# One order string of steps against another in a two-context, twelve-block kernel

## What is computed

```
for level in 0..3:
    x = x + cross_attention_level(norm(x), context)     # L0x, L1x, L2x, L3x
    x = attention_level(norm(x))                        # L0a (linear), L1a (softmax, band), L2a (linear), L3a (gated scan)
    x = x + experts_level(norm(x))                      # L0f, L1f, L2f, L3f (routed experts; L2f has an attention inside)
```

## Time and profile before

| | |
|---|---|
| Median of three runs | 2558.8 us (2552.28 to 2561.77) |
| Span of the profiled execution | 2557.4 us |
| Mean granted TensorE clock | 0.971 |
| PE busy / PEld busy | 2254.9 / 1506.9 us |
| DVE / ACT / POOL busy | 1746.6 / 1368.6 / 774.0 us |
| DMA | 84.14 MB, 33 GB/s |

### The profile page before, as it was taken

The page is one execution under the profiler, slowest core; times in us unless marked ns, Lnnn a source line. Parts: engine busy times, 40 slices in busy tenths (PEclk is TensorE's granted clock), DMA queues, the critical chain, the costliest instruction groups (busy, mean ns, idle before and its releaser), DMA issues.

```text
span 2557.4 us, 62072 instructions
## 1 busy us (share of the span) xinstructions
PE 2254.9 (88%) x26420; PEld 1506.9 (59%) x26556; DVE 1746.6 (68%) x4832; ACT 1368.6 (54%) x2287; POOL 774.0 (30%) x676
## 2 busy tenths in 40 slices
PE   5889999877988888998888888888988889999999
PEld 3556666655565554565655666665656556555666
DVE  5775666577667777676777778777767674556642
ACT  4667676545555665545666544344455544555542
POOL 3323446432342212122222122211223223323443
PEclk9999999989999999999999999999999989999999
DMA  3011313100000000010000000000000102121132
GB/s 115 19 41 34 80 45 75 42 24 9 9 11 14 8 8 6 1 47 10 17 16 10 19 25 25 25 16 17 10 11 16 58 8 71 40 55 54 55 104 62
DMA packets 50452, 84.14 MB, mean 33 GB/s; under 512 B 9536, under 2 KB 24768, under 8 KB 49792
## 3 DMA queue, kind: packets, MB, share of 16 engines
q1 hardware_dynamic: 50176, 80.18, 11.3%
HBM read 77.54 MB, written 2.62 MB: 31 GB/s over the span
## 4 chain that ended last, share of the span: by engine, by line
PE 57%; DVE 25%; ACT 8%; issue 4%; POOL 3%; DMA 1%; SPq 1%; another core or an unknown queue 0%; DVEq 0%; POOLq 0%; ACTq 0%
PE psum L946 6%; PE psum L908 5%; PE psum L904 5%; PE psum L1606 3%; PE psum L463 2%; DVE c_L3x_most L1726 2%; PE psum L1699 2%; DVE c_L2x_mx L2081 2%; PE psum L1984 2%; DVE c_L2x_p L2087 1%; PE psum L471 1%; PE psum L1395 1%; PE psum L1976 1%; PE psum L773 1%; PE psum L778 1%
## 5 line engine op out<-in xcount | busy, mean ns | idle before, releaser
L893 POOL TENSOR_TENSOR c_L3f_h<-c_L3f_h,c_L3f_spread 128x512 f32<-128x512 f32 x96 | 121.3, 1283 | 188.8 <-DMA c_L3f_spread<-scratch 103.1
L471 PE MATMUL psum<-halves_held 128*128 128x512 bf16 x454 | 131.0, 403 | 14.0 <-issue 9.8
L936 DVE TENSOR_TENSOR c_L3f_h<-c_L3f_h,psum 128x512 f32<-128x512 f32 (+1 forms) x112 | 75.9, 682 | 76.5 <-PE psum L908 52.0
L922 ACT ACTIVATE c_L3f_h<-psum 128x512 f32<-128x512 f32 (+1 forms) x112 | 65.5, 594 | 110.2 <-PE psum L904 99.1
L946 PEld LDWEIGHTS psum<-weights,c_L3f_h 128*128 128x128 f32 (+1 forms) x896 | 108.1, 193 | 19.3 <-issue 15.3
L946 PE MATMUL psum<-weights,c_L3f_h 128*128 128x128 f32 (+1 forms) x896 | 112.9, 279 | 0.0
L904 PE MATMUL psum<-c_L3f_xT,weights 128*128 128x512 f32 x208 | 107.4, 601 | 0.0
L908 PE MATMUL psum<-c_L3f_xT,weights 128*128 128x512 f32 x208 | 107.4, 603 | 0.0
L471 PEld LDWEIGHTS psum<-halves_held 128*128 128x128 bf16 x588 | 54.3, 102 | 74.8 <-issue 35.1
L893 POOL TENSOR_TENSOR c_L0f_h<-c_L0f_h,c_L0f_spread 128x512 f32<-128x512 f32 x64 | 82.5, 1313 | 50.4 <-DVE c_L0f_h L936 39.2
L1606 PE MATMUL psum<-c_L3x_qx,c_L3x_kT 32*128 32x256 f32 x512 | 77.1, 427 | 21.1 <-DVE c_L3x_most L1726 17.4
(11 more groups left out here) (640 smaller groups left out, 6520.0 us busy)
## 6 DMA issues: line engine op xcount, KB each, us to landing
c_L0f_spread<-scratch SPq DMA_DIRECT2D x64, 256.0 KB, 5.5
c_L3f_spread<-scratch SPq DMA_DIRECT2D x32, 512.0 KB, 5.3
c_L2f_spread<-scratch SPq DMA_DIRECT2D x64, 128.0 KB, 3.1
c_L3f_spread<-scratch SPq DMA_DIRECT2D x64, 128.0 KB, 5.8
c_L0x_ctxT<-ctxT SPq DMA_DIRECT2D x8, 384.0 KB, 7.8
c_L1x_ctx<-ctx SPq DMA_DIRECT2D x16, 192.0 KB, 2.4
c_L2x_ctxT<-ctxT SPq DMA_DIRECT2D x8, 384.0 KB, 3.6
c_L3x_ctxT<-ctxT SPq DMA_DIRECT2D x8, 384.0 KB, 3.7
```

Source lines behind the costliest of these rows:

```text
L471: nc.tensor.matmul(j.psum[:, bank, :], j.half["ident"], j.half["take"], start=True, stop=True)
L893: nc.gpsimd.tensor_tensor(h, h, j.m["spread"][:, f, :], ALU.mult).then_inc(*j.up("mixed"))
L922: nc.scalar.activation(j.m["h"][P - rows:P, f, :], j.psum[0:rows, 1 + 2 * f % 3, 0:j.tok], ACT.Silu).then_inc(*j.up("silu"))
```

## The change

The string `ORDER` is replaced by another one, and nothing else. Both strings hold the same 8114 steps and the same 9 `+`. The new one is joined from 25 stretches, each taken from one of three orders: the old one and two that were found by search. The digits differ: the old string asks for 588 fillers in all, the new one for 558.

Read step by step, both strings come again and again to the same state (the same steps issued). Between such states the queues' orders differ in ten parts of the run, by the profile's time of the old kernel: 0 to 152 us (L0x, L0a), 251 to 412 (L0f, L1x), 460 to 547 (L0f, L1x, L1a), 933 to 1164 (L2x, L1f, L2a), 1191 to 1219 (L2f, L2x), 1293 to 1392 (L2f, L2x), 1455 to 1540 (L2f, L2a), 1655 to 1822 (L3x, L2f), 2048 to 2064 (L3a, L3x) and 2120 to 2431 (L3f, L3x, L3a). Elsewhere they are the same. The place in its own queue changes for 458 of 2448 steps of PE, 374 of 1520 of ACT, 1180 of 3306 of DVE, 190 of 664 of POOL and 19 of 176 of SyncE; for 402 of PE's 458 by one or two places, for 16 of SyncE's 19 by one. Of the early steps that only do norms, 113 of DVE stand further ahead among the main steps than before and 123 further behind; of POOL 33 ahead and 23 behind. The fillers of the ten parts number 252 before and 222 after (0 to 152 us: 53 and 47; 460 to 547: 25 and 20; 933 to 1164: 68 and 57; 1455 to 1540: 10 and 16).

The diff replaces nearly every line of the string, since a shift of one letter moves all that follow. Its first lines:

```diff
 ORDER = (
-    "vqQDDddDVdldkdddp8paglPLaDKQqDpDDLPaApgApGp7PvvdDavAkGKvvpPPP1paVVa3pgdAdaVpgdVlVPp1pA2PGvQvA4PDadvAkPGPlPvdvkV1pVa3pDDA"
...
+    "vdDqDddldkqQdddplVDaL2pDaKQDdDDPpPagA1pgApLkpvGvD3PaAGvvVvpPaPKPg1paVAd5pagVdVdVPpAppvPlAlvda4PDAGQPGkvd5PvvD1PkVDpLVaAd"
...
```

More of the change, by code:

```diff
@@ L2845 @@
[L2845 to L2848, removed]
@@ L2909 @@
[L2909 to L2910 removed]
+    "vdDqDddldkqQdddplVDaL2pDaKQDdDDPpPagA1pgApLkpvGvD3PaAGvvVvpPaPKPg1paVAd5pagVdVdVPpAppvPlAlvda4PDAGQPGkvd5PvvD1PkVDpLVaAd"
+    "dDdvvlavdpavvaK1pVVvVP1PAApvvGkPvAlvG3PvQvvdPgPVvV9pgADDaDLaaVVaVPppppDapAppKDDDLDpQvvpPaAapaPaKpAPkdvvdvvdlGGvdlpvvPvPv"
+    "VVAvvvgVVvVkPA6PApDagDPApGpPaGaPPVpVDpAQLDppaaVKVVPpApvdDDDvpPaALvvapavGPvaLAG4pkPvDPdpvvPvVvVAvKVvVvVgPvVA1pgaVAVDPVApV"
@@ new lines @@
+    "ddAl+pdKDPpVpaaDPkpVVDaVLpapDVKVpVvVvGpLVa4pdPDpbArdrpKrdrlrPrrrGPrrrPrrArPArAPrArrPrrPaPVdvVPcApbPsaDVsVApAVsADpVDsvpLP"
+    "savgpVpgaPvgcVVgVpVcaVkcVpVGcVpvPaDpgApKvLPgaPGPPAAPAPAPPVDVPpApPaVVAcAAcpKDVVvDgPvgcVcPv1pVVVaVpVpbVpVdGpaDrLrVpavPGrpA"
+    "rrrLPrdrrPDrArrPKrrDdrlPrrAPrrrAvPAPPacVbVPpAspKDvPsaVsDVADpdsLAVpAVspvDgPagpVgpaKvgPcVgkVVpVcaVpVcVGcVcvGPvpAgPagPPALAP"
+    "pAAPPPvPVgVPAcVAVDPVAcVAcvpadPpbppalpaPpKDDVrrrdrdrrrrrrrvVrrVpvrarpVpvrrapVpvrrrapVpVVDcvbpGapVapvPGdsApvLDapqkPPAPAPsK"
@@ new lines @@
+    "PgAPAsgPPgVcsgcVcDPgsdAdcgvcgPBc+gRRdcDRRRlcRdRRRPRAvPRRRPRpkRaVPRRpdRRRapAPVCddBdpalvAagdDpvSPaVPkgvAPvvPVAPVPSAPgVPLvA"
+    "PSGPvPppapGSaaGCASqpGCvGvCVVGCadCGDvCGCKvCVPdApavdPDBldpdRaRRPRRpRkvpDaRPdpdvRdaRpRDRlaRpRRRgqRRRARpRavPaVCBgPAvvPVAPVPS"
+    "APgPvApvdpadpaddaPVklVSpPvGvdPSGPdavLvCSApGavPGVkSpGaPApGVDvppadAdGvapapagqpPaVCgvKCvGvdCCCCglvC1pvdpadpaV1PakApv1PvdPDd"
+    "avPlPvBpavDRRRRApRdaRRRPRRpRkRVvpapvapRRdaddpRRaRdRARRDlpqVCgaPBvAgPvPvLAVdPdSdPVAPgPvA2pvpaVdpaaPSV1pGPvvPlSaPvGvCSApGa"
@@ new lines @@
+    "vCkGdDSCGdpkaVCGpvpKGaPpAVapddapGdaqlpdvCdgdvCaCgCvvVPAgDPdDPBDRPRRLvARvplpaRpRaPdRaRVkpRRRARPvPRRvRaPDRVRPRRvRvCdApBaPS"
+    "vkpSapSvppaVApqdaddlpaSdgVpavGSvPGaPAgPvCAvdkgPdKVCdVPPlAvvpGpdapaPaGpAGCvGCvVaCGCvvCpaPvkpa1pvppadqdapvddVpaGpagvlCaVPA"
+    "gvvPdBRPRRPdAQdPgkAPv1pvpaVdpaald1pPvvPVDDaDvPLvDRRARRpdavRPRRkVpRARaRRpvppadKRRpRaddRaRpDagRVplvDPvaCBgPAvPvAVPVDPSAPgP"
+    "vApvpapaaSpPvGvSGaCvdLCvVSpGDavCGkSpGaCpGvKpGdDdaCVvpGpvCvCvCvVppgDPDPAgVvPvPvQdaVAApAGPvgAplvV1pGaVVpaapGVdpvkVvv4pv6PP"
@@ new lines @@
+    "APvAApvDpLaPVDpDVaDDpaLKpAvvvvVDV7pv+pPaKpVpAvpvPvAvgPdgpddvV4PPAaDPQvDPvVADpAAPvGADvpLGDpaDgpVDaDVLaVpGpv3plvVvv5PvAvpV"
+    "pPaDdPApAa1PapVpVAvkvvVv7pDVvpPaKpVKpvAvPvAvPgV1PpQDAgpPvPavDPvVApAAPvDvpLgDpaADGpGVadapVdpVGv3pDvvDvLV3PvPAvpdVplaPApAa"
+    "1PapVpVAvDdvkvv6pDVVvpPaApVpvPvAKvPpKvgVPQvgAPDPDDvaLPpDvdApAAPvGKvpdpVaDAdpDlVaGapVVdpGv3pvvVDvL3PvgPDvpVpaPApAAa1PapVp"
+    "VAvvkvVv9pVPvADpVavdKpvvvPaavvAvvPvvvvdvvvdvVPPAAPlvQDPvAvvDvDpvLAPaGDvdpAvKVpGVVpVaDGkvDpapVVPPDvApgPvpLaAgApPvagpVpVvA"
@@ new lines @@
+    "pDgpVVpvvvpPaApKVvvvPDaavvA1PvvvvvdvvvVPPAAPvQvPvAvvvGDpPDavAvDdLvVVpADvvpGVpVaGpapVvpVgPvPAPADpgaDADdlpadPkvgpVpVLvApgp"
+    "KVDVpDvvvpPaKpVAvvvPdaavvAvdPvvvvvvvvdVPPAAPlvQvvPvAvvVGvDpAPavVDpAvDpGLVpDVvaGDpapVdDVPpAvPDgvPApALakgPpVapVvApDgpKVVDP"
+    "vAgpVKPpAPVPAvvvpPPAaPADqGPADVdpVADddvGvvalVavvVvGvvvvvvvvvvvvvLVp1PvaVDvpvAvPPdApAPapVvVpApvaVgVKppkvgPaApVaPvgpApvPgpV"
+    "+DPpVADp2PvvPVvVqpVVGPapPVGvVApVDvLagPv1pVaVPg3PdnAPzmAzzPwy6nwwAdPyVny2nVxVPdzlzV2mVG1nxVmzxmwzw3mzPyw7PwwAnxP3mynxymnx"
@@ new lines @@
+    "2mAzznwDAPzKPw6mzVVVVwPzwVPAyPwPdVxnVPyVmVGnxDVGymDVx2mAnPww1mDzLzV4nGwPwwzx7mzzVy5nxVPDymnxmynwPwzzApPakpAvpAqddPaPpvdV"
+    "l1PgVvpVa4pVVagKnVPz1PmAzPzAwyPww6nxAmyPxnVy2nmzzdVnxVVmz1PwzwzVPmAyPwwVnwPyVxnPVVGymDnVGxzDz4nVAVmzPx4mzzPDwyLw1mVGnwPy"
+    "wwnyVxn3PzzAmnxPzmx1mzAww2mAzPywPw4nwVx1PVVVymVnxymV1nxkmDzPwwzpPaKpvpAqddPaApvgApPaPvpVadVlVmVngw2PzwdwzzVPA2PPxPPVmyVx"
+    "nVmVyxGDnmVyDw2nGwzzVnVA1mzPwzwzwy8nVxVPPyAmxPmxnmyww1nzAzmAnwPwkPwzzDxLz8mVVVyGPVxnmyxVnmyVDwPwPnzAzmPwwAnPwAPzzKVzxVVV"
@@ new lines @@
+    "6myPxVnPDVyDmAnxymwn+wzVzVVPpAaAVVVVpVVVvVVVpVVVDVVaVpPAPpavVV2pvVagVLVDnmzzKPzAwwPdPywAddPVnxGPyVmAnyGxPmnAzxzPmVwwnGmz"
+    "zPwPzPVwPwGylPVxVVPnAmyDxDDVPVVmALAnVxVyV2mwnVgwVVzzVV2mVnwwwzzdxzVVVV7mVVVVVPVDyAnxPVmyxnmywVwPAmnwzzwPAwnPzzxPzVPVmGyx"
+    "PGAnAPymVxnyPmGnwzwzPVpaPGpkvPpdKdaPVvVvVPAapvvaDVVaV2PvAADVVVVVVVDVVdV6pVlvLVVdVVVVpVvPvAVvPVpVDaPkpvpaAPAPvavpaVvaPdGv"
+    "PAVKPGPAVpGPvPVdPGpdvvPlvdPpVaVVPApDkvVVPVpAAdVVaVVQVVVVVVVVVVVV6pVPvAvVVaPaVVvDDdPvLAdPladPkApvPVPVpGDvAvGPvAPpVPKaVGPp"
@@ new lines @@
+    "GvpadPPPVVvpvaVaddvlavlPDDVDddAQpLvPpvPvGAvpVaP+AVpkvNkpZZaMZpaWWpWvYapavpvvNXgvYMvpvXdNgMXY2MgWNZZWpddppllpG7NvvvaZpMva"
+    "ZWaZppvYvpv2NvvvWvpvYDvWpKNvgXvvgv8pYvapMrrrbrprXrrNrrrMrrprZrpaXcvpbaMspWdvdaZW1MksNsWpWpvWpagpavgcgZcgZcvcXcvpaMZpavXa"
+    "ppYpvvNMgXvavYvpMWgWNYg1MNWpWpWZZppXv2NvaZvZpvaMaZpYpvXvNvvpYvMvNXvvMY1NkWvpZWZP1pAPvgvvVPgQv2pAa2pGprrPrbrrddpraPprArpr"
+    "arPdrlrrrvcAdvvbpVspapaVskvsNMZppZaZggcvYWgcgcDlcvDcWWvpNaXppvaaYpMvpXvNgvMY2NXvaMZgZ1NWWvDpgZMLZZpGpWYp7NWWDXp2MvYvNXYv"
@@ L2913 @@
+    "PSPASpVPPAapVvpaGbPsLPAGPVDpvGsPaGApsVPGvPAsGPVPASgCVgCsPPASPVPApVCCpPpAGaPvGPVpAgaPKgPVvPGACVgPpGCaGACVgCCGCgCgCCCVSPpA"
+    "pPaPRvPRRgBRRpRRpRARvCgPBaSpApvSVPgPVSpAaPSvPVgPASGPVPAGPVGPAPGVPAGPVPGAPVGPAGPVPAGPVPGApVpGapvPaPvAPVPGAPVcAVcccccccccc"
+    "cccCvsCCCCCCCCCCCCCVS")
 class Flow:
```

97 lines of the change are left out of this document (32 added, 65 removed).

## The result

The new kernel takes 2544.89 us (median of 4 runs, 2538.89 to 2546.96), the old one beside it 2560.13 (2552.28 to 2561.77): a ratio of 0.9935, 95% interval 0.9915 to 0.9954. In a later comparison (six runs of the new kernel, thirteen of the old one) it was 0.9949, 0.9929 to 0.9969. So the new order saves 13 to 17 us.

What follows compares the result with a forecast made beforehand. TensorE's queue was taken to set the pace (busy 2254.9 of 2557.4 us), then VectorE, with no transfer mattering. Terms -2.7 - 1.2 - 1.9 - 3.4 - 0.9 + 0.5 - 5.0 = -14.6 gave 2544 us; range 2522 to 2566.

Steps and rivals of the forecast that it cites:

- The hole at 993 us: 4.09 us wait of PE; two routing steps go ahead of the key spreads on DVE: -2.7, its clock -1.2.
- The hole at 2222 us: 1.88 us hole; a DVE step goes ahead of the product that releases POOL: -1.9, and -3.4 of clock.
- The hole at 2336 us: 3.00 us hole of PE; it only changes its owner, with the normalizing step 0.9 us earlier: -0.9.
- rival 1: Whole run: the holes come back a step later, no change, 2554 us; chance 0.22.
- The hole at 136 us: 8.20 us wait of PE for x_held; two norm operations leave DVE's queue ahead, L584 starts later: net +0.5.
- The small holes: 100 us of holes in nine changed parts, mostly under 1.5 us each: 5% taken, -5.0.
- The clock: Low-clock stretches behind the holes at 993 and 2222 us: -1.2 and -3.4.
- The fillers: 588 before, 558 after; 30 fewer are at most -7.1, but they mostly cost nothing: 0 taken.
- Rival 3: All parts gain, with a fifth of the small holes and a third of the clock: -39, 2520 us; chance 0.20.
- Rival 4: Fewer fillers at 490, 1000, 1200 and 1700 us, so the clock falls: slower, ten falls 2578 us; chance 0.11.
- those at L1431, L1532 and L1734: About 990 us: wait 1.3 us or less, L1532 starts before second L1768 ends; L3x6: L1734 0.18 us, 1.88 wait gone.
- those at L904, at L463 of L0a3: L3a5: wait of 2 to 3 us at L904, not L463; L0a3: the 8.20 us before L463 become 8 to 9.

Runs made afterwards that it cites:

- DVE's edit: Old order with three edits alone (routing steps ahead of a key spread on DVE at 993 us, one DVE step at 2221, three PE steps at 2336): ratio 0.9969.
- the one edit: Old order with one DVE step moved at 2221 us, 1 L3x6 v23 ahead of 0 L3f1 v11: single run 2547.09 us.
- that one edit: Old order with three PE steps moved at 2336 us, 0 L3f3 p16, c3, p17 ahead of 1 L3a5 p9: single run 2554.08 us.
- picked parts: Old order with the new order in five parts (0 to 151, 460 to 547, 933 to 1163, 1293 to 1392, 2119 to 2431 us): ratio 0.9942.

## Why the prediction was right, and where it was not

The forecast was 2544 us, -14.6; measured 2544.89, -15.2 between the medians and -13.1 between the two profiles. The total was good, its terms less so: that it came within 1 us is luck, since much of the 24.5 us lay in parts of which no term speaks, and 9 of them were taken back.

1. *The hole at 993 us* (-2.7, and -1.2 of clock). The size is near: 3.2 us are gained up to the second group of L1984, with the clock at 1.00, and the part at 933 us gave 1.5 to 3.1 us in all. The way there is another. The step failed that says "the cast then ends at about 995.0", 0.3 us behind v18: where DVE's edit stands alone, the cast is kept by POOL's second spread as v18 is by the first (1.82 us for 0.20), and 2.81 us of the wait are left. It also took the time of the keys for fixed. In the new kernel they come later, nothing is locked out, the whole wait goes, and 1.92 us come back at L1976.
2. *The hole at 2222 us* (-1.9 and -3.4 of clock). Right in mechanism, and in size within the scatter: the one edit gave 2.9 to 4.4 us for 5.3.
3. *The hole at 2336 us* (-0.9). The step failed that says "p16 waits for the product v6". I had counted PE's steps wrongly: p16 is the gate projection of the eighth tile and waits for the sixth product, v5, which ends at 2332.1 in the profile of that one edit, ahead of the four L384 (2332.66). The fill went through as the string says. That it still brought only 0.4 to 1.9 us is rival 1 at this place.
4. *The hole at 136 us* (+0.5). It is 7.97 for 8.20 us, a little less and not more. The step failed that has L615 wait for the root behind L713: in the new trace the root is done and L615 starts at 123.86, 2 us ahead of L713. And the part gained 6.7 us, none of which I saw: L584 starts at 128.03 for 134.81, so that the gain was made ahead of the largest hole, the only one at which I had looked.
5. *The small holes* (-5.0). This is the term of which I knew least. The parts at 22 and 460 us gave 12 in these profiles (some 9 over all profiles) and that at 2119 us more than my terms 2 and 3 (9.7 for 6.2); the unchanged parts took 9 back. The sum fell near -5 by compensation, and not because a twentieth was the right share.
6. *The clock* (-4.6 in the terms above). Each single low stretch that I named did go, but the sum of half clock over the run is the same, and so is the mean, 0.971.
7. *The fillers* (0). The term was put at nothing; in the new order the new fillers are worth 3 to 6 us, a quarter or more of the forecast, and in the old order they cost 10. The step that failed is "they stand in front of waits, so that they mostly cost nothing": they cost or save by the order in which they stand.
8. "The parts outside the ten keep their lengths within 1 us each" was wrong, by 2.6 to 3.8 us in three of them. At 547 and 1822 us that is no more than scatter from one execution to the next. At 1538 us it is the hole without a releaser and the low clock behind it, which go with the fillers ahead.

Rival 3, all parts gaining, failed on the part at 251 us (1.4 us longer), on those at 1192 and 1656 us, which gained nothing beyond scatter, and on the unchanged ones. (Its half-way point to the forecast is 2532 and not 2530.) Rival 4, clock lost for want of fillers, fits the old order with the new fillers (+10 us, at a mean clock of 0.967 for 0.971 and 0.973) and did not happen in the new.

Of the signs that were to show the prediction right, those at L1431, L1532 and L1734 came true; those at L904, at L463 of L0a3 (7.97 us, for 8 to 9) and for the unchanged parts did not. Neither of the two that were to show it wrong came: the parts at 251 and 2119 us gained 8.2 us together and not over 10, and the mean clock is 0.971.

## What to carry to other kernels

When an order is joined from stretches, the gains of the stretches do not add up: here 24.5 us in the changed parts left 13 to 17, and 27 us of picked parts left 15. The last part, behind which TensorE is busy for 123 of 126 us, kept its gain. Two profiles are too few for a gain of 5 us in a part with a scatter of 4. A small operation of VectorE with two SBUF inputs just behind the release of a GpSimd operation took until that operation's end here, and so did a cast with one; put it ahead of what releases GpSimd. Fillers belong to the order in which they were tuned and have to be set anew with it.

## What the runs showed of the hardware that was not expected

- A cast of 128x64 with one SBUF input (L1532, 0.195 us in all eight of its instances before) took 1.82 us beside a GpSimd operation.
- Keys spread on VectorE and GpSimd together took 4.66 us on VectorE; started behind GpSimd, the same two operations took 1.40.
- 558 fillers of about 0.24 us, some 130 us of TensorE, save 80 us net: without them the mean clock is 0.914 for 0.971.
- Two executions of one kernel differ by up to 2.6 us in a part of 99 us, and kernels with the same queues up to there by 4.5 us in one of 87.
- TensorE stands still for 1.9 to 2.5 us in a run of short matmuls without a wait (L2299 and L2306 at about 1579 us), in the six profiles with changed fillers ahead of it and in none of the seven with the old ones.
